# Between two transformer layers: batch 0's expert results are loaded first and added one by one, and TensorE projects batch 0 before it sums the other batches

## The chip, the cores and the metric

The kernel runs on one core of one Trainium2 chip, as a single program. The metric is the device time of that program in microseconds (us). Five engines run their own instruction streams in order and meet at semaphores: TensorE (PE in the profile, with its weight loads as PEld), VectorE (DVE), ScalarE (ACT), GpSimd (POOL) and SyncE (SP), which only issues DMAs here. ACT and POOL issue DMAs too; DMAs of one issuing engine go into one queue.

## The reference

Two layers over 4 batches of 512 tokens with 256 channels, all in float32. Each layer normalises the tokens and adds attention and a mixture of experts to them:

```
x = L0_attn_hidden_states                         # [4, 512, 256]
xn = _layernorm(x)
x = x + attn0(xn) + ffn0(xn)    # 16 experts, top 4 of a softmax, plus a shared expert
xn = _layernorm(x)
x = x + attn1(xn) + ffn1(xn)    # 32 query heads of 8 channels on 8 key groups; 7 experts, top 3, plus a shared one
```

In layer 1 the fused projection of `xn` gives 256 query, 64 key and 64 value columns; each of the 8 groups has one key head of 8 channels, which serves 4 query heads: scores over 512 keys, softmax, weighted values.

## The kernel before, in words

Tokens live in `x`, 16 tiles of 128 tokens by 256 channels, four tiles to a batch. Products of two float32 operands are made from a high part and a remainder (`_hi`, `_lo`) in three matmuls (`mm3`, L543 to L546). Layer 0 ends with the routed experts: POOL scatters their weighted results, one row for each token and choice, into the DRAM tensor `yk[0]`, four choices k = 0 to 3 of 2048 rows each. Then comes the stretch that the change is about. The order in every engine's stream is written out by hand; nothing is scheduled.

**Loads of the results.** For each batch b, SP issues choices 0 and 1 (`load_results`, L347 and L365 to L367) and ACT choices 2 and 3 (L1167 to L1170) into `yg[0][b]`: 16 DMAs of 512 KB, eight in each queue, batch 0 first. All four of a batch count on one semaphore, `m_yg[b]`.

**Adding them to the tokens.** `combine0(b, bank)` (L1524 to L1536) does it on DVE. Batch 0 takes four adds of 128 x 1024 elements, after all four loads have landed. For batches 1 to 3 DVE adds choice 0, TensorE adds up choices 1 to 3 with identity matmuls in two PSUM banks (`sum_results`, L912 to L919, 6 matmuls), and DVE adds the banks to the tokens (L1321). In TensorE's stream `sum_results(1)` stands ahead of the transposes of batch 0, `sum_results(2)` ahead of its two first projections and `sum_results(3)` behind them (L921 to L931).

**Normalising.** For each batch DVE takes moments (`moments`, L1283 to L1289), POOL a power (`root`, L437), DVE five small steps (L1296 to L1300), ACT writes four normalised tiles (`normalised`, L1007), TensorE transposes them (`tokens_t`, 8 transposes at L553, into the banks of `xt_bank`), ACT casts the high part (`high_parts`, L997) and DVE the remainder (`low_parts`, L1307).

**First projections and keys.** `project(2, 0)` gives batch 0's keys and values, `project(0, 0)` the queries of groups 0 to 3 (six matmuls each, L544 to L546). `compact` copies them out on ACT (L1186 to L1191) and DVE (L1673, L1676). SP then copies keys and queries inside SBUF into the form in which the scores want them: `stack_keys(u)` is four DMAs of 24 rows (L380) and `stack_queries(u)` one of 96 rows (L393), for each unit u, which is one key group of one batch.

**Units.** `stage(b, s)` is written once for each engine. Stage (0, 0) is the first unit of batch 0: 16 score matmuls (L815), each followed by a maximum on DVE (`reduce_max`, L1721) that frees its bank; a score waits for the maximum of the third score before it. Between these 16 steps stands what the dictionary `early` names for a step: in stage (0, 0) the transposes of batches 1 to 3, the last projection of batch 0 (`project(1, 0)`), `combine0`, `moments`, `root` and `low_parts` of batches 1 to 3. Behind the 16 steps follow the gate logits of all four batches (`logits`, six matmuls each, copied out by ACT and transposed in `logits_by_token`, L570); DVE takes them (`take_logits`, L1316), and then the second unit, stage (0, 1), begins with its first score. From there on units follow each other to the end of layer 1's attention, then its experts.

Of the kernel before, what the change touches and what calls it, by code (L numbers as in the profile page):

```python
# [41 lines left out]
def program(nc, x_in, aw0_in, aw1_in, ws0_in, moe0_in, moe1_in, pad_in, const_in, bias_in, out):  # L42
# [3 lines left out]
    with ctx:  # L46
# [179 lines left out]
        m_yg, m_fin = [sem(f"m_yg{b}") for b in range(B)], sem("m_fin")  # L226

# [17 lines left out]
        def batches(l, n):  # L245
            return n + l * B
# [76 lines left out]
        def _(sp):  # L323
# [23 lines left out]
            def load_results(l, b, k):  # L347
                r = k * T + b * S
                sp.dma_start(yg[l][b][:, k], yk[l][r:r + S, :].rearrange("(p t) h -> p t h", t=QT)).then_inc(m_yg[b], 16)
# [15 lines left out]
            for b in range(B):  # L365
                load_results(0, b, 0)
                load_results(0, b, 1)  # L367

            def stack_keys(u):
# [9 lines left out]
                for r in range(R):  # L379
# [45 lines left out]
        def _(pool):  # L425
# [61 lines left out]
            def add_results(b):  # L487

                pool.wait_ge(m_yg[b], 16 * (TOP0 + TOP1))
# [52 lines left out]
        def _(pe):  # L542
# [369 lines left out]
            def sum_results(b, bank):  # L912

                pe.wait_ge(m_yg[b], 16 * TOP0)
                for c in range(2):
                    for k in range(1, TOP0):
                        ins = nc.tensor.matmul(psum[:, bank + c, :], ident, yg[0][b][:, k, 2 * c:2 * c + 2, :],
                                               start=(k == 1), stop=(k == TOP0 - 1))
                ins.then_inc(m_ps, 1)  # L919

            sum_results(1, 4)  # L921
            tokens_t(1, 0)
            sum_results(2, 6)
# [4 lines left out]
            pe.wait_ge(s_ve, B + 2)  # L928
            sum_results(3, 4)
            pe.wait_ge(b_hi, 1)  # L930
            tokens_t(1, 1)  # L931
# [4 lines left out]
            def first_values():  # L936
# [3 lines left out]
            stage(0, 0, False, {1: lambda: pe.wait_ge(s_xl, 2 * B + 4), 3: last_projection, 7: lambda: tokens_t(1, 2),  # L940
                                11: lambda: tokens_t(1, 3), 12: first_values})
            pe.wait_ge(s_xl, 2 * B + 8)
            for b in range(B):
                logits(1, b, psum[:, 4 + b, :])
# [50 lines left out]
        def _(act):  # L995
# [171 lines left out]
            for b in range(B):  # L1167
# [53 lines left out]

            normalised(1, 0)
            high_parts(1, 0)
            normalised(1, 1)
# [664 lines left out]
```

## Time and profile before

| | us |
|---|---|
| runs shown | 1116.78, 1118.92, 1118.95 |
| median of the runs | 1118.92 |
| the profiled execution, its own time | 1118.09 |
| its span, first to last instruction | 1116.3 |
| from the first load of results to the first score of unit 0 | 384.57 to 423.01 |
| from that score to the first score of unit 1 | 423.01 to 457.74 |

All times of the trace are us from the start of the span. In a row of the timeline the first two numbers are start and duration, then engine, line of the kernel, operation, what it writes and reads, how many were merged, and in brackets how long the engine had been idle and what ended that. An engine that is idle costs nothing unless what it does next is waited for; so a stretch is read from its end backwards, always to what released it last.

### The profile page before, as it was taken

How to read it: one execution, taken by the hardware profiler on the slowest of the kernel's cores; microseconds unless marked ns; L12 is line 12 of the kernel's file. 1: busy time of each engine (PE TensorE's matmuls, PEld its weight loads, DVE VectorE, ACT ScalarE, POOL GpSimd, SP SyncE). 2: the span in 40 equal slices, each digit the busy share in tenths (PEclk: the TensorE clock that was granted, in tenths of full speed). 3: DMA queues.
4: the chain of work that ended last, by engine and by line, in shares of the span. 5: the costliest groups of instructions: out<-in, count | busy, mean ns of one | idle time of the engine just before them, and what ended most of it. 6: DMA issues, size and time to landing. Idle time of an engine off the chain costs nothing.

```text
span 1116.3 us, 17223 instructions
## 1 busy us (share of the span) xinstructions
PE 1004.6 (90%) x5701; PEld 735.6 (66%) x5701; DVE 762.9 (68%) x1575; ACT 591.3 (53%) x894; POOL 315.5 (28%) x330
## 2 busy tenths in 40 slices
PE   4999998789999575999999999999999987999996
PEld 3877876689999533555545555555555565888885
DVE  6577556566655257799898888888888756444438
ACT  6325553565555453466655665666566655444431
POOL 2004777256744400000000122222221000455432
PEclk9999998899999886999999999999999998999998
DMA  6863333655344352121111222222222124333244
GB/s 235 308 277 127 104 128 110 206 160 157 122 135 134 129 238 34 18 34 28 22 29 29 44 57 58 57 57 57 57 57 44 64 83 149 110 106 105 86 175 174
DMA packets 48962, 120.20 MB, mean 108 GB/s; under 512 B 7736, under 2 KB 24760, under 8 KB 48344
## 3 DMA queue, kind: packets, MB, share of 16 engines
q1 hardware_dynamic: 18960, 66.15, 20.3%
q0 software_dynamic: 11760, 32.24, 7.6%
q10 hardware_dynamic: 18160, 20.71, 6.5%
q8 instruction: 51, 0.84, 0.3%
q14 instruction: 31, 0.25, 0.1%
HBM read 72.17 MB, written 52.29 MB: 111 GB/s over the span
## 4 chain that ended last, share of the span: by engine, by line
PE 66%; DVE 14%; POOL 6%; ACT 5%; DMA 4%; issue 3%; SPq 0%; ACTq 0%; DVEq 0%; POOLq 0%
PE psum L815 11%; PE psum L837 10%; PE psum L824 8%; PE psum L630 5%; PE psum L631 4%; PE psum L632 4%; POOL xg L462 4%; DVE work_f L1721 4%; PE psum L544 3%; PE psum L545 3%; PE psum L546 3%; PE psum L616 2%; PE psum L641 2%; ACT work_f L1214 1%; DVE x L1321 1%
## 5 line engine op out<-in xcount | busy, mean ns | idle before, releaser
L1721 DVE TENSOR_REDUCE work_f<-psum 128x1 f32<-128x512 f32 x512 | 334.9, 685 | 51.1 <-PE psum L815 49.7
L1214 ACT ACTIVATE work_f<-psum 128x1024 f32<-128x1024 f32 x172 | 168.9, 1023 | 111.9 <-PE psum L824 110.3
L815 PE MATMUL psum<-work_r 128*128 128x512 f32 x512 | 205.3, 440 | 20.0 <-DVE work_f L1721 7.1
L469 POOL DMA_INDIRECT yk<-yb,dest x133 | 129.2, 971 | 238.7 <-ACT yb L1060 209.9
L815 PEld LDWEIGHTS psum<-work_r 128*128 128x128 f32 x512 | 94.2, 190 | 131.5 <-DVE work_f L1721 75.8
L824 PE MATMUL psum<-qm,work_r 128*128 128x512 f32 x512 | 161.8, 398 | 4.2 <-ACT work_f L1214 2.7
L462 POOL DMA_INDIRECT xg<-xn,slot x112 | 108.3, 967 | 180.5 <-PE psum L853 152.3
L824 PEld LDWEIGHTS psum<-qm,work_r 128*128 128x128 f32 x512 | 93.6, 188 | 31.8 <-ACT work_f L1214 10.9
L630 PE MATMUL psum<-wexp,xbh 128*128 x266 | 101.6, 382 | 9.3 <-issue 4.3
L1214 ACT ACTIVATE pt<-psum 128x1024 f32<-128x1024 f32 x84 | 82.8, 1023 | 50.2 <-PE psum L824 49.3
L631 PE MATMUL psum<-wexp,xbh 128*128 x266 | 95.7, 360 | 0.0
L632 PE MATMUL psum<-wexp,xbl 128*128 x266 | 95.2, 358 | 0.0
L837 PE MATMUL psum<-work_f 128*32 128x512 f32 x688 | 89.1, 602 | 0.6 <-ACT work_f L1214 0.6
L1044 ACT ACTIVATE sgb<-psum 128x352 f32<-128x352 f32 (+1 forms) x67 | 34.6, 517 | 97.5 <-PE psum L632 94.1
L1492 DVE TENSOR_TENSOR xbl<-psum,xbh 128x512 fp32r<-128x512 f32 x67 | 46.0, 686 | 57.5 <-ACT xbh L997 57.5
L1060 ACT ACTIVATE yb<-psum,share 128x256 f32<-128x256 f32 x133 | 55.9, 471 | 47.6 <-PE psum L659 23.8
L458 POOL TENSOR_TENSOR xn<-const 128x16 f32<-128x16 f32 x7 | 1.5, 218 | 260.2 <-PE psum L853 186.3
L1503 DVE TENSOR_TENSOR hb<-sgb,psum 128x352 f32<-128x352 f32 (+1 forms) x67 | 39.0, 582 | 51.9 <-ACT sgb L1044 51.9
L630 PEld LDWEIGHTS psum<-wexp,xbh 128*128 128x128 f32 x266 | 51.5, 194 | 15.6 <-issue 11.9
L632 PEld LDWEIGHTS psum<-wexp,xbl 128*128 128x128 f32 x266 | 51.6, 194 | 5.0
L631 PEld LDWEIGHTS psum<-wexp,xbh 128*128 128x128 f32 x266 | 51.6, 194 | 3.7
L616 PE MATMUL psum<-const,xb 128*128 128x128 f32 x266 | 41.3, 278 | 12.4 <-DVE xbl L1492 8.3
(218 smaller groups left out, 2035.3 us busy)
## 6 DMA issues: line engine op xcount, KB each, us to landing
xb<-xg ACTq DMA_DIRECT2D x62, 258.0 KB
xg<-in_pad SPq DMA_DIRECT2D x1, 10320.0 KB
yg<-yk SPq DMA_DIRECT2D x20, 512.0 KB, 9.3
stage<-in_moe SPq DMA_DIRECT2D x16, 608.0 KB, 5.2
xg<-in_pad SPq DMA_DIRECT2D x1, 7224.0 KB
work_r<-work_r SPq DMA_DIRECT2D x128, 48.0 KB
work_r<-work_r SPq DMA_DIRECT2D x32, 192.0 KB
stage<-in_moe SPq DMA_DIRECT2D x16, 384.0 KB, 3.8
```

What stands on the lines that cost most here:

```text
L462: nc.gpsimd.indirect_dma_start(xg[l], bass.IndirectOffsetOnAxis(ap=slot[l][:, at:at + 1], axis=0), xn[l][:, t, :], None).then_inc(m_scat, 16)
L469: nc.gpsimd.indirect_dma_start(yk[l], bass.IndirectOffsetOnAxis(ap=dest[:, j % 8, i:i + 1], axis=0), yb[l][:, j % 2, i, :], None).then_inc ...
L616: ins = nc.tensor.transpose(psum[:, 4, (i * KH + c) * P:(i * KH + c + 1) * P], xb[l][:, j % 2, i, c * P:(c + 1) * P], ident)
L630: nc.tensor.matmul(o, xbh[l][:, j % 2, i * KH + c, :], hi, start=c == 0, stop=False)
L631: nc.tensor.matmul(o, xbh[l][:, j % 2, i * KH + c, :], lo, start=False, stop=False)
L632: ins = nc.tensor.matmul(o, xbl[l][:, j % 2, i * KH + c, :], hi, start=False, stop=c == KH - 1)
L815: nc.tensor.matmul(next_bank(pe, ("scores", n), b_mx, n + 1), qs[g % 2][:, t * P:(t + 1) * P], km[g % 4][:, r, :], start=True, stop=True). ...
L824: ins = nc.tensor.matmul(psum[:, 3 + 2 * h + r % 2, :], km[g % 4][:, r, t * P:(t + 1) * P], qm[g % 2], start=True, stop=True)
L837: ins = nc.tensor.matmul(psum[32 * r:32 * r + 32, 7, :], va[:, t, g % NG * 32:g % NG * 32 + 32], pt[(n * QT + t) % 3][:, r, :], start=(t = ...
L1060: ins = nc.scalar.activation(yb[l][:, j % 2, i, :], psum[:, 6 + j % 2, i * H:(i + 1) * H], ACT.Identity, scale=share[:, j % 8, i:i + 1])
L1214: nc.scalar.activation(pt[((b * NG + g) * QT + t) % 3][:, 2 * h:2 * h + 2, :], psum[:, 3 + 2 * h:5 + 2 * h, :], ACT.Exp, scale=float(HD) * ...
L1721: v.reduce_max(mx[:, s % 2, i:i + 1], ring["scores", n], AX.X).then_inc(b_mx, 1)
```

## The change

SP and ACT issue the four loads of batch 0 with a semaphore for each choice (`m_y0[k]`). SP waits for choice 0 of them, and then issues all twelve loads of batches 1 to 3 itself. DVE adds batch 0's four in the order 0, 2, 1, 3, each when it has landed (`combine_first`). TensorE transposes and projects batch 0 first; then, for each of the other batches, it adds the tokens and all four choices in PSUM, in two halves of five identity matmuls (`sum_half`), and ACT copies the sum back over the tokens (`take_sum`), so DVE adds nothing for them. Batch 1's halves stand behind the projections, those of batches 2 and 3 between the scores of unit 0. Two of the four key copies of the first unit are issued by ACT. The logits move from behind unit 0 to its steps 13 and 15, except those of batch 3.

```diff
-            return ((0, 2), (3, 0), (6, 7), (4, 5))[b][k] if layer == 1 else 2 * b + k
+            return ((0, 2), (4, 5), (6, 7), (4, 5))[b][k] if layer == 1 else 2 * b + k
...
-            for b in range(B):
-                load_results(0, b, 0)
-                load_results(0, b, 1)
+            load_results(0, 0, 0)
+            load_results(0, 0, 1)
+            sp.wait_ge(m_y0[0], 16)
+            for b in range(1, B):
+                for k in range(TOP0):
+                    load_results(0, b, k)
...
-                for r in range(R):
+                for r in range(R if u else 2):
...
+            def sum_half(b, bank, c):
                 pe.wait_ge(m_yg[b], 16 * TOP0)
+                tokens = slice(b * QT + 2 * c, b * QT + 2 * c + 2)
+                nc.tensor.matmul(psum[:, bank + c, :], ident, x[:, tokens, :], start=True, stop=False)
+                for k in range(TOP0):
+                    ins = nc.tensor.matmul(psum[:, bank + c, :], ident, yg[0][b][:, k, 2 * c:2 * c + 2, :],
+                                           start=False, stop=(k == TOP0 - 1))
+                if c == 1:
+                    ins.then_inc(m_ps, 1)
...
+            def sum_last(c):
+                pe.wait_ge(s_xl, 2 * B + 4)
+                sum_half(3, 4, c)
...
-            stage(0, 0, False, {1: lambda: pe.wait_ge(s_xl, 2 * B + 4), 3: last_projection, 7: lambda: tokens_t(1, 2),
-                                11: lambda: tokens_t(1, 3), 12: first_values})
+            stage(0, 0, False, {0: lambda: sum_half(2, 6, 0), 1: lambda: sum_half(2, 6, 1), 2: lambda: tokens_t(1, 1),
+                                3: last_projection, 4: lambda: sum_last(0), 5: lambda: sum_last(1),
+                                7: lambda: tokens_t(1, 2), 10: lambda: tokens_t(1, 3),
+                                12: first_values, 13: first_logits, 15: third_logits})
...
-            for b in range(B):
-                for k in (2, 3):
-                    r = k * T + b * S
-                    act.dma_start(yg[0][b][:, k], yk[0][r:r + S, :].rearrange("(p t) h -> p t h", t=QT)).then_inc(m_yg[b], 16)
+            for k in (2, 3):
+                act.dma_start(yg[0][0][:, k], yk[0][k * T:k * T + S, :].rearrange("(p t) h -> p t h", t=QT)).then_inc(m_y0[k], 16)
...
+            def take_sum(b, bank):
+                act.wait_ge(m_ps, sums(0, b))
+                copy(x[:, b * QT:(b + 1) * QT, :].rearrange("p t h -> p (t h)"),
+                     psum[:, bank:bank + 2, :].rearrange("p c n -> p (c n)")).then_inc(s_cp, 1)
...
+            def combine_first():
+                dve.wait_ge(f_y, batches(0, B))
                 dve.wait_ge(s_xb, TT)
+                for k in (0, 2, 1, 3):
+                    dve.wait_ge(m_y0[k], 16)
                     noted()
+                    note(v.tensor_tensor(x[:, 0:QT, :], x[:, 0:QT, :], yg[0][0][:, k], ALU.add))
                 noted()
...
-            stage(0, 0, False, {1: lambda: low_parts(1, 1), 2: lambda: combine0(2, 6), 3: lambda: moments(1, 2),
-                                4: lambda: root(1, 2),
-                                6: lambda: combine0(3, 4), 7: lambda: moments(1, 3), 8: lambda: root(1, 3),
-                                9: lambda: compact(1, 0, psum[:, 3, :], 2), 10: lambda: low_parts(1, 2),
-                                13: lambda: low_parts(1, 3), 14: lambda: values_by_key(0, psum[:, 3, :])})
+            stage(0, 0, False, {0: lambda: summed_moments(1), 1: lambda: root(1, 1), 3: lambda: low_parts(1, 1),
+                                4: lambda: summed_moments(2), 5: lambda: root(1, 2),
+                                6: lambda: compact(1, 0, psum[:, 3, :], 2), 7: lambda: summed_moments(3),
+                                8: lambda: root(1, 3), 9: lambda: low_parts(1, 2),
+                                12: lambda: low_parts(1, 3), 14: lambda: values_by_key(0, psum[:, 3, :])})
```

TensorE's stream from the end of layer 0's experts to the first score, before (L917 is a sum of results, L553 a transpose of batch 0 or 1, L544 to L546 the projections, L815 a score):

```order
L917 MATMUL psum<-yg_1_129,const 128x512 [waits m_yg1,m_y]
L917 MATMUL psum<-yg_1_129,const 128x512 x5
L553 MATMUL psum<-const,xn_71 128x128 [waits s_xn]
L553 MATMUL psum<-const,xn_71 128x128 x7
L917 MATMUL psum<-yg_2_130,const 128x512 [waits m_yg2]
L917 MATMUL psum<-yg_2_130,const 128x512 x5
L544 MATMUL psum<-xt_hi_67,aw_73 128x512 [waits s_xl,s_split]
L545 MATMUL psum<-xt_lo_69,aw_73 128x512
...
L917 MATMUL psum<-yg_3_131,const 128x512 [waits m_yg3,s_ve]
L917 MATMUL psum<-yg_3_131,const 128x512 x5
L815 MATMUL psum<-work_r_146 128x512 [waits b_qd,b_kd]
```

The same place now (L558 transposes, L549 to L551 project, L921 and L923 are the sums, L820 a score):

```order
L558 MATMUL psum<-const,xn_71 128x128 [waits s_xb,s_xn,f_y,m_y]
L558 MATMUL psum<-const,xn_71 128x128 x7
L549 MATMUL psum<-xt_hi_67,aw_73 128x512 [waits s_xl,s_split]
L550 MATMUL psum<-xt_lo_69,aw_73 128x512
...
L921 MATMUL psum<-x,const 128x512 [waits m_yg1]
L923 MATMUL psum<-yg_1_129,const 128x512 x4
L820 MATMUL psum<-work_r_146 128x512 [waits b_qd,b_kd]
L921 MATMUL psum<-x,const 128x512 [waits m_yg2]
L923 MATMUL psum<-yg_2_130,const 128x512 x4
L820 MATMUL psum<-work_r_146 128x512
L558 MATMUL psum<-const,xn_71 128x128 [waits s_xn]
```

The sums moved from ahead of batch 0's transposes and projections to behind them, and batches 2 and 3 into unit 0. ACT's stream from the loads on, now (L1188 loads results, L1017 casts or copies, L1027 normalises, L1204 to L1209 copy projections out, L1252 copies keys):

```order
L1188 DMA yg_0_128<-yk 128x1024 [waits m_st1,m_st0,s_split]
L1207 ACTIVATE work_f_147<-psum,bias 128x512 [waits b_pj]
L1209 ACTIVATE work_r_146<-psum,bias 128x512 x2
L1204 ACTIVATE work_r_146<-psum,bias 128x512 [waits b_pj]
L1204 ACTIVATE work_r_146<-psum,bias 128x512
L1252 DMA work_r_146<-work_r_146 24x1x512 [waits b_km,b_lo]
L1252 DMA work_r_146<-work_r_146 24x1x512
L1017 COPY x<-psum 128x1024 [waits m_ps]
L1027 ACTIVATE xn_71<-x,rs 128x256 [waits s_nm]
L1027 ACTIVATE xn_71<-x,rs 128x256 x3
L1017 COPY x<-psum 128x1024 [waits m_ps]
```

Before, the four normalised tiles of batch 1 stood ahead of the first of these copies of projections (L1007 ahead of L1189); now they stand behind both, behind the two key copies and behind the first copy of a sum.

## Rows read from the trace of the kernel before

**Rows 1.** The page, part 2: busy tenths of TensorE, 40 slices of 27.9 us

```profile
PE   4999998789999575999999999999999987999996
```

**Rows 2.** Busy time by stretch: us, each engine's busy (instructions), granted TensorE clock, DMA share, GB/s

```profile
392.87:397.88 5.01, 0.00 (x0) 0.03 (x1) 4.90 (x4) 4.41 (x3) 0.00 (x0) 0.50 1.02 417
397.88:401.40 3.52, 3.52 (x4) 1.48 (x5) 2.23 (x11) 0.00 (x0) 1.04 (x1) 0.50 1.04 425
...
429.10:444.00 14.90, 6.59 (x18) 3.29 (x16) 13.29 (x40) 6.47 (x12) 2.01 (x2) 0.72 0.11 15
444.00:449.70 5.70, 5.65 (x20) 4.56 (x21) 5.35 (x10) 1.17 (x2) 0.00 (x0) 0.52 0.00 0
449.70:457.70 8.00, 6.99 (x38) 5.49 (x36) 1.42 (x5) 3.62 (x5) 0.00 (x0) 1.00 0.00 0
```

**Rows 3.** Timeline from the loads of results to the projections of batch 0

```profile
384.57 4.13 SPq L349 DMA_DIRECT2D yg<-yk  x8
...
392.87 5.00 DVE L1531 TENSOR_TENSOR x<-x,yg 128x1024 f32<-128x1024 f32 x4 [16.02 <-DMA yg<-yk]
...
397.88 7.26 PE L917 MATMUL psum<-yg,const 128*128 128x512 f32 x12 [20.02 <-DMA yg<-yk]
...
402.08 2.08 ACT L1007 ACTIVATE xn<-x,rs 128x256 f32<-128x256 f32 x4 [4.79 <-DVE rs L1300]
...
404.98 1.04 PE L553 MATMUL psum<-const,xn 128*128 128x128 f32 x8
...
406.44 1.29 DVE L1307 TENSOR_TENSOR xt_lo<-psum,xt_hi 128x512 fp32r<-128x512 f32 x2
...
410.61 0.80 PE L544 MATMUL psum<-xt_hi,aw 128*128 128x512 f32 x1
...
413.80 5.31 PE L917 MATMUL psum<-yg,const 128*128 128x512 f32 x12
```

**Rows 4.** SP's loads of results: issue to landing; then GB/s in the first 20 us (40 slices)

```profile
DMA to landing us min/median/max: 4.5/11.9/18.5
...
GB/s 0 0 0 66 246 303 377 410 426 426 385 377 426 401 409 413 413 409 503 399 466 433 389 357 412 430 418 412 350 41 0 0 0 0 0 0 0 0 0 0
```

**Rows 5.** Timeline from the first copies of projections to the first score

```profile
413.76 0.66 ACT L1189 ACTIVATE work_f<-psum,bias 128x512 f32<-128x512 f32 x1
...
415.61 0.69 DVE L1676 TENSOR_TENSOR work_r<-work_f,work_r 128x512 fp32r<-128x512 f32 x1 [3.87 <-ACT work_r L1191]
416.33 2.93 SPq L380 DMA_DIRECT2D work_r<-work_r  x4
...
419.35 0.64 SPq L393 DMA_DIRECT2D work_r<-work_r  x1
...
423.01 1.19 PE L815 MATMUL psum<-work_r 128*128 128x512 f32 x2 [3.03 <-DMA work_r<-work_r]
```

**Rows 6.** Timeline of unit 0 to the first score of unit 1

```profile
427.20 0.63 PE L545 MATMUL psum<-xt_lo,aw 128*128 128x512 f32 x1
...
427.63 0.63 PE L546 MATMUL psum<-xt_hi,aw 128*128 128x512 f32 x1
...
429.40 1.39 DVE L1283 BATCH_NORM_STATS2 st<-x 128x6 f32<-128x256 f32 x4
...
433.52 2.07 ACT L1007 ACTIVATE xn<-x,rs 128x256 f32<-128x256 f32 x4 [12.86 <-DVE rs L1300]
...
435.65 1.97 PE L553 MATMUL psum<-const,xn 128*128 128x128 f32 x8 [0.71 <-ACT xn L1007]
...
444.05 1.97 PE L553 MATMUL psum<-const,xn 128*128 128x128 f32 x8 [0.76 <-ACT xn L1007]
...
448.42 0.79 PE L544 MATMUL psum<-xt_hi,aw 128*128 128x512 f32 x1
...
457.74 0.97 PE L815 MATMUL psum<-work_r 128*128 128x512 f32 x3 [0.37 <-DVE lg L1316]
```

**Rows 7.** The page, part 5: ScalarE on 128 x 1024 elements out of PSUM

```profile
L1214 ACT ACTIVATE work_f<-psum 128x1024 f32<-128x1024 f32 x172 | 168.9, 1023 | 111.9 <-PE psum L824 110.3
```

More of the change, by code:

```diff
@@ L226, in program @@
         m_yg, m_fin = [sem(f"m_yg{b}") for b in range(B)], sem("m_fin")
+        m_y0, s_cp = [sem(f"m_y0_{k}") for k in range(TOP0)], sem("s_cp")
         def pairs(l, n):
@@ L348, in load_results @@
                 r = k * T + b * S
[L349 removed]
+                landed_on = m_y0[k] if l == 0 and b == 0 else m_yg[b]
+                sp.dma_start(yg[l][b][:, k], yk[l][r:r + S, :].rearrange("(p t) h -> p t h", t=QT)).then_inc(landed_on, 16)
             for e in range(9):
@@ L908, in sequence @@
                     stage(b, s, last)
-            def sum_results(b, bank):
+            def sum_half(b, bank, c):
                 pe.wait_ge(m_yg[b], 16 * TOP0)
[L915 to L921, printed above, removed]
+                tokens = slice(b * QT + 2 * c, b * QT + 2 * c + 2)
[5 more added lines that the diff above has]
+                    ins.then_inc(m_ps, 1)
+            pe.wait_ge(f_y, batches(0, B))
+            pe.wait_ge(s_xb, TT)
             tokens_t(1, 0)
-            sum_results(2, 6)
             pe.wait_ge(s_split, SPLIT_A1)
@@ L927, in _, with first_logits, third_logits @@
             project(0, 0, psum[:, 2, :])
[L928 to L931, printed above, removed]
+            sum_half(1, 4, 0)
+            sum_half(1, 4, 1)
+            def sum_last(c):
+                pe.wait_ge(s_xl, 2 * B + 4)
+                sum_half(3, 4, c)
+            def first_logits():
+                pe.wait_ge(s_xl, 2 * B + 6)
+                logits(1, 0, psum[:, 6, :])
+                logits(1, 1, psum[:, 7, :])
+            def third_logits():
+                pe.wait_ge(s_lt, B + 1)
+                logits(1, 2, psum[:, 6, :])
             def last_projection():
@@ L1233, in _ @@
             for b in range(B):
-                logits(1, b, psum[:, 4 + b, :])
+                logits(1, b, psum[:, 6 + b % 2, :])
             stage(0, 1, False)
@@ L1522, in routed, with summed_moments @@
                     weights(j)
-            def combine0(b, bank):
-                dve.wait_ge(f_y, batches(0, b + 1))
+            def combine_first():
+                dve.wait_ge(f_y, batches(0, B))
                 dve.wait_ge(s_xb, TT)
-                dve.wait_ge(m_yg[b], 16 * TOP0)
-                tiles = slice(b * QT, (b + 1) * QT)
-                for k in range(1 if b else TOP0):
+                for k in (0, 2, 1, 3):
+                    dve.wait_ge(m_y0[k], 16)
                     noted()
-                    note(v.tensor_tensor(x[:, tiles, :], x[:, tiles, :], yg[0][b][:, k], ALU.add))
-                if b:
-                    dve.wait_ge(m_ps, sums(0, b))
-                    noted()
-                    note(add_to_tokens(tiles, bank))
+                    note(v.tensor_tensor(x[:, 0:QT, :], x[:, 0:QT, :], yg[0][0][:, k], ALU.add))
                 noted()
+            def summed_moments(b):
+                dve.wait_ge(s_cp, b)
+                moments(1, b)
             def combine1(b):
@@ L1651, in _ @@
             dve.wait_ge(a_y, B + 1)
-            combine0(0, 0)
+            combine_first()
             moments(1, 0)
             root(1, 0)
-            combine0(1, 4)
             low_parts(1, 0)
-            moments(1, 1)
-            root(1, 1)
             def value_columns(c0, c1):
```

15 lines of the change are left out of this document (11 added, 4 removed).

## The prediction, made before the changed kernel ran

> **What bounds the kernel now.** I read the busy tenths first. TensorE is busy nearly everywhere; the dip to 5, 7 and 5 in slices 14 to 16 (363 to 446 us) is where the change is [rows 1]. Next I read the timeline of that dip, backwards from the first score of unit 1 at 457.74, which waits for DVE to take the gate logits [rows 6]. What feeds it is a chain through every engine. Results land, the last after 392.87; DVE adds batch 0 until 397.87; ACT normalises from 402.08; TensorE transposes at 404.98, and DVE's remainders end at 407.73. But the projections start only at 410.61, as twelve sums of batch 2 stand ahead of them [rows 3]. ACT copies the first one out only at 413.76, behind its normalising of batch 1; four key copies take SP from 416.33 on, the query copy goes out at 419.35, and the first score starts 3.66 later [rows 5]. Then unit 0 takes 34.7 us, with the last transposes at 444.05 and the logits from 448.42 on [rows 6]; DVE is busy 13.29 of 14.90 us there, TensorE 6.59 [rows 2]. So DVE and the chain of one batch after another bound that part, not TensorE.
>
> **Part 1: loads and adds.** Batch 0's transfers stand first in both queues already. SP's quickest result landed 4.5 us after its issue [rows 4]; three more of 0.524 MB at the 417 GB/s that flow there [rows 2] take 3.8, together 8.3, and the first add starts 392.87 - 384.57 = 8.3 after the first issue [rows 3]. So sending batch 0 out alone is worth nothing (bounds 0 and 1 us). What gains is that the adds no longer wait for all four. The add of choice 0 can start at about 389.4, and that of choice 2 follows. The first two end at 391.9. The last result lands at 392.87; when the third lands no row shows, and after it two adds of 1.25 remain. So the end is between 394.1 (one add left after 392.87) and 395.4 (two). I take 394.7, which is 3.2 earlier than 397.87.
>
> Batches 1 to 3 now come through SP's queue alone, issued from about 389.3, when SP's new wait for choice 0 ends; only these loads stand behind that wait. Twelve issues of 0.52 us [rows 3] take 6.2. SP's queue alone carried 380 to 430 GB/s in the kernel's first microseconds [rows 4], so 6.3 MB need 15 us: batch 1 is there by 398, batch 3 by 408, before anyone wants it.
>
> **Part 2: to the first projections.** From the last add to ACT's first normalised tile it takes 402.08 - 397.87 = 4.21, the four tiles 2.08 [rows 3]: 401.0. The transposes then start at once, where before they stood 0.8 behind the sums. But those sums had warmed TensorE. After its idle 20 us the granted clock was 0.50, the lower level of 1.2 GHz, and still so over the first four sums [rows 2]; now the transposes come first. At that level eight transposes take 1.97 [rows 6] and not 1.04 [rows 3]. Before, 2.75 passed from their start to the end of the remainders; I take 3.3. The projections start at 404.4, not at 410.61.
>
> Twelve projections cost (413.80 - 410.61) = 3.2 us at the full clock [rows 3], and 0.43 each, 5.2 in all, at half clock (427.20 to 427.63) [rows 6]. TensorE has hardly run until then, so I take half clock but for the last few: the first six end at 407.1, the second six at 409.3. At the full clock throughout, the first score would come 2 us sooner.
>
> The Trainium skill ("TensorE: Matmul & The Clock Gate", section "Part 1: The HAM clock gate") says that the array is throttled by default and that activity releases it. That speaks against putting the sums last, and by that rule, with which the row at 0.50 agrees, the slow prices above stand; without it the sum would come out about 2.5 us earlier.
>
> **Part 3: keys, queries, first score.** ACT no longer has batch 1's tiles ahead. From its start to DVE's compaction it is 415.61 - 413.76 = 1.85, then 0.69 [rows 5]: keys are ready at 409.7, not 416.3. SP issues two key copies (half of 2.93) until 411.2; the queries need ACT's copies of the second projection (1.25) and 0.75 on DVE: 411.4. The first score follows 3.66 after the query's issue [rows 5]: 415.1, which is 7.9 earlier than 423.01. ACT's own two issues (1.5 us, from 410.6) end at 412.1, before the sum that ACT waits for next.
>
> In TensorE's stream batch 1's ten sums stand ahead of that score: 0.44 each at full clock (5.31 for 12) [rows 3], 4.4, so 409.4 to 413.8. The wait for the queries hides them; at the 0.88 of the first four sums [rows 2] they would end at 418.2 and cost 3.1.
>
> **Part 4: unit 0.** DVE loses four passes of 1.25 over batches 2 and 3, and gains moments and root of batch 1, about 3 us. TensorE gains twenty sums (8.8 us) between scores. ACT gains three copies, 1.02 each by [rows 7], and batch 1's four tiles. DVE's moments now wait for ACT's copies, and behind them on DVE stand the maxima that free the scores' banks; so scores and sums of a later batch wait too. One batch hangs on the other: ACT's copy of the sum, then 433.52 - 429.40 = 4.12 from the moments to the first tile, 2.07 for the tiles, then transposes, casts, remainders [rows 6]. Batch 1: copy until 414.9, tiles 419.0 to 421.1; batch 2's sums end at about 420. Batch 2: ACT copies at 421.1 to 422.1, casts until 423.3, DVE's remainders until 424.6, then moments; tiles 428.7 to 430.8. Batch 3's ten sums wait for batch 1's remainders, 424.5 to 429 with their scores. ACT copies the last projection (1.25) and then this sum, until 433.1; moments from 433.6, tiles 437.7 to 439.8. So the last transposes start at 439.9, 4.2 before 444.05: of the 7.9 us, 3.7 go back.
>
> **Part 5: tail.** From the last transposes to unit 1 it was 13.7, of which 24 logit matmuls took 6.3 from 448.42 on [rows 6]. Now: transposes 1.97, three scores and the values 1.7, twelve logits 3.15, two scores 0.5, twelve logits 3.15, copy 0.7, then 2.34 as before: 453.3. With the first twelve at half clock, as the last transposes ran (clock 0.52) [rows 2], it is 455.3. I take 454.0 against 457.74: **3.7 us earlier**. Behind it nothing is changed, so the shift is carried to the end.
>
> The profiled execution took 1118.09, which gives 1114.4. The median of the runs is 0.83 higher, so I predict **1115.2**. With 0.7 either way in part 1, 2 us of clock in parts 2 and 3 and 2 in part 5, of which unit 0's chain hides some, its own range is 1113.0 to 1117.5.
>
> **Rivals.**
>
> *Slower: TensorE stays at 1.2 GHz.* Unit 0 has it idle for long (6.59 of 14.90 us busy, clock 0.72) [rows 2], and the change puts more matmuls on the chain. At half clock all through: batch 1's sums end at 418.2 and the first score stands there; batch 2's sums end near 428, its copy and batch 1's transposes behind them, batch 3's sums near 440.5, last transposes near 449.9, and the tail takes some 19 with 10.4 for the logits: 469, or 12 us slower, 1131. It decides from about 4 us of such losses on: batch 3's sums at half clock (4.4) alone eat the gain, 1119.9. Against it: the sums themselves keep TensorE busy, and before the change the transposes behind twelve of them already ran at the fast price (1.04) [rows 3]. Chance 0.09.
>
> *No change: given back in unit 0.* If unit 0 hangs wholly on ACT and DVE, the earlier first score is worth less than I think. ACT has batch 1's and 2's tiles, two copies and the last projection in one line; one more wait of a tile set (2.07) behind a copy or a maximum leaves 1.6 us: 1117.3. For it: DVE's 13.29 of 14.90. Chance 0.20.
>
> *The loads come late.* With SP's queue at half the rate, 6.3 MB would last until 420, and the keys and queries of unit 0 stand behind them in that queue: first score at 423 as before, and the unit 3.7 longer: 1122.6. Rows 4 speak against it. Chance 0.03. The Trainium skill ("DMA: Bandwidth & Descriptors", section "Queues, rings and completion order") says that every DMA engine takes turns between the queues that have work. Batch 1's loads, issued while choices 1 and 3 still flow, would then take turns with ACT's choice 3; no row here shows a queue that joins late, and the cost would fall inside the 1 us in which I let the third and fourth land.
>
> *More: the clock comes up early and stays.* The 2 us of part 2, 0.7 of part 1 and the fast tail add up to a first score of unit 1 at 451 or before: 1112 or less. Chance 0.07.
>
> **How the numbers follow.** The forecast has 0.61, the rivals 0.09, 0.20, 0.03 and 0.07. About 0.2%, 2.2 us, is what a measurement of this kernel can tell from none. Faster: nine tenths of the forecast (0.55), all of the large gain (0.07) and a third of the second rival (0.07): 0.69. Slower: 0.03, three quarters of the first rival (0.07) and a little of the second (0.01): 0.11. The rest, 0.20, is the same. From 1112.3 to 1119.0 leaves out the late loads, most of the half clock and the largest gains, not quite 2 in 10.
>
> **What would show it.** In the profile of the changed kernel, in each case against the times above: the last add of batch 0 near 394.7; the projections near 404.4 and at 0.43 apart at first; the first score near 415, released by a DMA inside SBUF; last transposes near 440, that is 25 us after the first score and not 21; unit 1 near 454; and everything behind it shifted by as much. I am wrong on the mechanism if the first score waits for sums or for loads, and on the size if the last transposes come 21 us or 29 us after it.

## The result: slower by 0.4%, and the profile after

The changed kernel takes **1122.65 us** (median of 19 runs, 1118.14 to 1128.49), the kernel before 1118.30 in the same comparison (19 runs). The ratio is 1.0039 with an interval of 1.0027 to 1.0052. Forecast were 1115.2 us and 3.7 us of gain; measured are 4.4 us of loss.

The profiled execution of the changed kernel, 1128.49 us, is the longest of its 19, so its stretches are read one by one and not its total. Counted from the first load of layer 0's results, which shuts out what layer 0 does before it, the profiles of before and after say (us):

| | before | forecast | after |
|---|---|---|---|
| last add of batch 0 | 13.3 | 10.1 | 10.2 |
| transposes of batch 0 start | 20.4 | 16.4 | 16.6 |
| projections start | 26.0 | 19.8 | 20.1 |
| first key copy issued | 31.8 | 25.1 | 25.6 |
| first score of unit 0 | 38.4 | 30.5 | 33.4 |
| last transposes (batch 3) | 59.5 | 55.3 | 62.3 |
| first score of unit 1 | 73.2 | 69.4 | 75.3 |
| from there to layer 1's first load of results | 620.5 | 620.5 | 620.3 |
| from that load to the end | 38.0 | 38.0 | 43.4 |

The span is 10.3 us longer: 3.0 ahead of the first load, where nothing is changed, 2.15 up to unit 1, -0.2 in the long middle, and 5.4 at the end. The 2.15 and the 5.4 have each a cause of their own. That is more than the 4.4 us of the medians, so the terms are those of one execution.

The rows that answer to [rows 3] and [rows 5] show the first half of the table. The timeline of VectorE and of TensorE after the change, with start, duration, engine, line, operation, tiles, count, and the idle time ahead with its releaser:

```profile
392.35 2.55 DVE L1560 TENSOR_TENSOR x<-x,yg 128x1024 f32<-128x1024 f32 x2 [13.38 <-DMA yg<-yk]
395.22 2.56 DVE L1560 TENSOR_TENSOR x<-x,yg 128x1024 f32<-128x1024 f32 x2 [0.31 <-DMA yg<-yk]
```

```profile
404.20 1.94 PE L558 MATMUL psum<-const,xn 128*128 128x128 f32 x8 [24.11 <-ACT xn L1027]
407.63 0.77 PE L549 MATMUL psum<-xt_hi,aw 128*128 128x512 f32 x1 [1.49 <-DVE xt_lo L1337]
408.20 0.63 PE L550 MATMUL psum<-xt_lo,aw 128*128 128x512 f32 x1
408.63 0.63 PE L551 MATMUL psum<-xt_hi,aw 128*128 128x512 f32 x1
```

The adds start 4.8 after the first load and wait only 0.31 between; the transposes take 1.94 and the projections start 0.43 apart, which is the half clock that was forecast. The next rows, TensorE's timeline of the sums of batches 1 and 2, show what was not:

```profile
412.75 1.02 PE L921 MATMUL psum<-x,const 128*128 128x512 f32 x2
...
413.61 3.60 PE L923 MATMUL psum<-yg,const 128*128 128x512 f32 x8
...
417.04 1.02 PE L921 MATMUL psum<-x,const 128*128 128x512 f32 x2
...
417.90 3.60 PE L923 MATMUL psum<-yg,const 128*128 128x512 f32 x8
...
420.94 0.79 PE L820 MATMUL psum<-work_r 128*128 128x512 f32 x1
...
421.57 1.02 PE L921 MATMUL psum<-x,const 128*128 128x512 f32 x2
422.42 3.60 PE L923 MATMUL psum<-yg,const 128*128 128x512 f32 x8
425.46 0.80 PE L820 MATMUL psum<-work_r 128*128 128x512 f32 x1
426.09 1.02 PE L921 MATMUL psum<-x,const 128*128 128x512 f32 x2
426.95 3.60 PE L923 MATMUL psum<-yg,const 128*128 128x512 f32 x8
429.98 0.79 PE L820 MATMUL psum<-work_r 128*128 128x512 f32 x1
430.61 1.04 PE L558 MATMUL psum<-const,xn 128*128 128x128 f32 x8
```

Batch 1's two halves have 5 matmuls each in the code (the tokens and four results) and 2 + 8 instructions each in the trace: a plain float32 matmul is **two** instructions, each 0.43 long at full clock. Ten sums are 20 instructions and 8.65 us, not 4.4. The first score stands behind them without an idle time of its own, each of the next two scores waits for a half of batch 2, and batch 1's transposes wait for all of it, until 430.61. The table of stretches (length, busy time and count of PE, PEld, DVE, ACT and POOL, clock, DMA share, GB/s) says the same against [rows 2]:

```profile
412.75:421.40 8.65, 8.65 (x22) 3.86 (x21) 2.71 (x6) 1.27 (x2) 0.00 (x0) 1.00 0.34 51
...
429.10:444.00 14.90, 14.90 (x54) 8.39 (x52) 8.36 (x24) 6.64 (x12) 1.01 (x1) 1.00 0.04 6
```

From 429.1 to 444.0 the kernel before had TensorE busy for 6.59 of 14.90 us and VectorE for 13.29 [rows 2]. Now TensorE is busy for all of it, at full clock, and VectorE for 8.36. TensorE has become the bound of this part of unit 0. The page's tenths [rows 1], slices of 28.2 us now, have slices 14 to 16 at 4, 5, 8 instead of 5, 7, 5: the two in which the first results land and are added (366 to 422 us) are emptier than before, that of unit 0 (422 to 451) is fuller. The last slice is at 5 instead of 6:

```profile
PE   4999998689999458999999999999999978999995
```

The second loss is at the end. These are stretches of 6 us in layer 1, 12 to 18 and 18 to 24 us behind its first load of results; first the kernel before, then the changed one:

```profile
1090.25:1096.25 6.00, 5.94 (x32) 4.93 (x31) 5.85 (x6) 1.12 (x2) 4.27 (x2) 1.00 1.00 406
1096.25:1102.25 6.00, 6.00 (x39) 5.34 (x38) 5.96 (x6) 1.12 (x2) 2.67 (x1) 1.00 0.03 12
```

```profile
1095.19:1101.19 6.00, 4.44 (x24) 3.35 (x23) 6.00 (x2) 0.00 (x0) 4.62 (x2) 1.00 0.83 340
1101.19:1107.19 6.00, 5.09 (x18) 4.22 (x19) 5.96 (x9) 2.21 (x4) 2.37 (x1) 0.72 0.22 89
```

VectorE is busy for the same 6 us, but in the first of the two stretches with two instructions instead of six; TensorE waits, then runs at a granted clock of 0.72. None of this code is changed, but for the counts of semaphores. What is changed is its neighbour: the trace's DMA records hold 16 KB fetches of instructions on queue 8, 51 before and 52 now. One falls 8.7 us behind layer 1's first load of results before, and 2.9 us behind it now. The second and third result then land at 5.45 and 7.21 us instead of 4.74 and 6.00, and GpSimd's first add starts at 7.3 instead of 6.07.

### The profile page after: what moved, and what is told of

It reads as the page before. It is cut to its first block, busy times and chain, and to the rows that moved or that the text cites. A ratio compares the mean times of both kernels' runs of the same rounds, so it can differ in the third digit from the quotient of the medians.

```text
span 1126.6 us, 17262 instructions
## 1 busy us (share of the span) xinstructions
PE 1012.8 (90%) x5725; PEld 739.7 (66%) x5725; DVE 757.9 (67%) x1569; ACT 594.8 (53%) x897; POOL 316.4 (28%) x330
## 4 chain that ended last, share of the span: by engine, by line
PE 67%; DVE 13%; POOL 7%; ACT 5%; DMA 4%; issue 4%; SPq 0%; ACTq 0%; DVEq 0%; POOLq 0%
PE psum L820 10%; PE psum L842 10%; PE psum L829 8%; PE psum L635 5%; PE psum L636 4%; PE psum L637 4%; POOL xg L467 4%; DVE work_f L1747 4%; PE psum L549 3%; PE psum L550 3%; PE psum L551 3%; PE psum L646 2%; PE psum L621 2%; PE psum L923 2%; DMA yg<-yk 1%
## 5 line engine op out<-in xcount | busy, mean ns | idle before, releaser
L820 PE MATMUL psum<-work_r 128*128 128x512 f32 x512 | 204.4, 437 | 10.4 <-DVE on L1718 4.9
L820 PEld LDWEIGHTS psum<-work_r 128*128 128x128 f32 x512 | 93.4, 188 | 120.6 <-DVE work_f L1747 69.0
L1232 ACT ACTIVATE pt<-psum 128x1024 f32<-128x1024 f32 x84 | 82.9, 1024 | 50.2 <-PE psum L829 49.3
```

The source lines that it names most:

```text
L820: nc.tensor.matmul(next_bank(pe, ("scores", n), b_mx, n + 1), qs[g % 2][:, t * P:(t + 1) * P], km[g % 4][:, r, :], start=True, stop=True). ...
L1232: nc.scalar.activation(pt[((b * NG + g) * QT + t) % 3][:, 2 * h:2 * h + 2, :], psum[:, 3 + 2 * h:5 + 2 * h, :], ACT.Exp, scale=float(HD) * ...
```

## The experiments

Two theories for the first loss: TensorE's row is too long (a sum costs twice what was counted), or the first unit hangs on VectorE and ScalarE. Two for the second: the place of the instruction fetch, or what the change computes. Each ratio is to the kernel before on the same chip; the differences of stretches are to the first profiles of the two kernels. Sums in the reduced type were not measured, so the price of a sum is tested by its place and by fewer sums alone.

**The changed kernel again, unaltered.**

> The changed kernel itself, to see what of its profile comes back. Theory A (a sum on TensorE costs 0.88 us and not the 0.44 that the prediction took, because a float32 matmul is two instructions): the first score again waits for batch 1's sums, about 30.3 us from the first score's wait-free time on, and from the first load of results to unit 1 about 75 us; the rest of the kernel as before the change. Then the time is 1119 to 1122. Rival B (something in the last 45 us, behind layer 1's experts, has become 5 us slower for good): the last stretch is 5 us longer in this profile too.

Measured: 1124.67 us, ratio 1.0049 (1.0032 to 1.0066). Unit 1 at 74.4 us behind the first load, the end stretch 43.4 again. Both losses repeat, the first one smaller: the first score comes at 32.7 and not 33.4, unit 1 1.2 us behind the kernel before and not 2.15 (the third profile, further down, has 32.8 and 74.4). The 3.0 us ahead of the first load do not repeat (1.1 here).

**The loads alone**: the kernel before with batch 0's loads sent out by themselves. The edit in short:

```
+ m_y0 = [sem(f"m_y0_{k}") for k in range(TOP0)]     # batch 0: one semaphore per choice
+ load_results(0, 0, 0); load_results(0, 0, 1); sp.wait_ge(m_y0[0], 16)
+ for b in range(1, B): all four choices by SP       # ACT loads only choices 2, 3 of batch 0
+ DVE adds batch 0 in the order 0, 2, 1, 3, each after its own semaphore
```

> The kernel before with the first part of the change alone: four semaphores for batch 0, its adds in the order 0, 2, 1, 3, and batches 1 to 3 loaded by SP. The step of the prediction on loads and adds: the last add of batch 0 ends 10.2 us after the first load instead of 13.3. Theory A says nothing more comes of it, because TensorE's sums of batch 1 stand ahead of batch 0's transposes and cannot start before batch 1 has landed: transposes within 0.5 us of before, time 1117.5 to 1119. Rival D (the earlier adds alone carry the gain): 3 us sooner at every later step, time 1115 to 1116.

Measured: 1119.82 us, ratio 1.0008 (0.9997 to 1.0020). The adds end at 10.2 us as in the changed kernel, yet the transposes start at 21.95 us instead of 20.4, later than even theory A allowed. TensorE's timeline of this kernel shows why:

```profile
399.03 7.78 PE L922 MATMUL psum<-yg,const 128*128 128x512 f32 x12 [21.06 <-DMA yg<-yk]
406.65 1.04 PE L558 MATMUL psum<-const,xn 128*128 128x128 f32 x8
407.52 5.32 PE L922 MATMUL psum<-yg,const 128*128 128x512 f32 x12
```

Batch 1's sums stand ahead of the transposes, and batch 1 lands 1.0 later behind the first load than before (the sums then take 7.78 instead of 7.26), so what the adds gain is lost again. Loads and order belong together.

**Batch 1 added by VectorE**: the changed kernel, with batch 1's four results added by VectorE while it waits for keys, and one half of batch 2's sum ahead of the first score.

```
- sum_half(1, 4, 0); sum_half(1, 4, 1)               # TensorE, ahead of the first score
+ sum_half(2, 6, 0)
- stage(0, 0, False, {0: sum_half(2, 6, 0), 1: sum_half(2, 6, 1), 2: tokens_t(1, 1), ...
+ stage(0, 0, False, {0: sum_half(2, 6, 1), 2: tokens_t(1, 1), ...
+ combine_second()                                   # DVE: four adds, after low_parts(1, 0)
```

> As the changed kernel, but batch 1's four results are added by DVE, 5 us in the time in which it otherwise waits for the copies of the first projection, and batch 1's moments follow those copies; TensorE does batch 2's first half where batch 1's sums stood. Theory A: 8.8 us of sums less on TensorE before the first score, one copy less on ACT; first score about 28 us after the first load, batch 1's tiles 8 us earlier, unit 1 at 67 to 70 us after the first load, time 1113 to 1116. Rival C: no gain over the changed kernel beyond 1 us, as DVE bounds unit 0.

Measured: 1118.30 us, ratio 0.9994 (0.9982 to 1.0005); unit 1 at 72.3 us, the end stretch 38.2, the fetch at 7.0 us. Ten matmuls fewer take unit 1 from 75.3 (74.4 in the other two profiles) to 72.3. That is short of theory A's 67 to 70, and so is the time; and of the gain over the changed kernel the end stretch has the larger part (5.2 us in the profiles). The first score was to come at 28 and came at 32.4, only 1.0 earlier, though TensorE stood idle ahead of it:

```profile
411.45 3.60 PE L923 MATMUL psum<-yg,const 128*128 128x512 f32 x8
418.67 0.47 PE L820 MATMUL psum<-work_r 128*128 128x512 f32 x1 [3.62 <-DMA work_r<-work_r]
418.98 1.18 PE L921 MATMUL psum<-x,const 128*128 128x512 f32 x2
419.96 5.17 PE L923 MATMUL psum<-yg,const 128*128 128x512 f32 x8
```

So the score waits for the query copy, and the second half of the sum stands behind the score when it could lie in that 3.62.

**Both halves ahead of the first score**: the kernel just told of, with the half moved into the gap.

```
  sum_half(2, 6, 0)
+ sum_half(2, 6, 1)
- stage(0, 0, False, {0: sum_half(2, 6, 1), 2: tokens_t(1, 1), ...
+ stage(0, 0, False, {1: tokens_t(1, 1), ...         # DVE's steps 3, 4, 5 one earlier
```

> Batch 1's results are added by VectorE, as in the run before it, and both halves of batch 2's sum now stand ahead of the first score, batch 1's transposes after the first score instead of the second. Theory (a sum costs TensorE 0.88 us, so a batch's ten sums 8.8 us, and whatever stands behind them in TensorE's row is late by what sticks out of the wait for the query): the 4.3 us of the second half fit into the 3.6 us in which TensorE waits for the query, so the first score is at most 0.7 us later, batch 1's transposes start 4 to 5 us earlier (about 34.5 us after the first load of results instead of 39.2), unit 1 at 68 to 70 us after that load instead of 72.3, and the kernel takes 1113.5 to 1116 us. Rival (the first unit is bound by VectorE's and ScalarE's work and not by TensorE's row): unit 1 stays at 72 us and the time at 1118 us.

Measured: **1111.61 us**, ratio 0.9952 (0.9935 to 0.9970), the fastest version. It beats the kernel before by 0.5% and the changed one by 0.9%, the latter in part by the end stretch (37.4 us). The first score is no later (32.4 us), unit 1 comes at 66.2, earlier than the theory's 68 to 70, and the time is below its range too:

```profile
413.05 1.02 PE L921 MATMUL psum<-x,const 128*128 128x512 f32 x2
413.91 3.60 PE L923 MATMUL psum<-yg,const 128*128 128x512 f32 x8
416.95 1.02 PE L820 MATMUL psum<-work_r 128*128 128x512 f32 x2
418.19 1.09 PE L558 MATMUL psum<-const,xn 128*128 128x128 f32 x8 [0.22 <-ACT xn L1027]
```

Batch 1's transposes start 33.7 us behind the first load; in the changed kernel it was 43.1. The 10 matmuls taken off TensorE and the place of five are worth 9.1 us at unit 1 (8.2 against the other two profiles): the theory of TensorE's row holds, the rival (72 us) falls.

**Two results fewer in each sum.**

```
-                for k in range(TOP0):
+                for k in range(2):
```

> The changed kernel with choices 2 and 3 left out of TensorE's sums of batches 1 to 3, so that three matmuls make a half instead of five (the results of these two choices are missing from those batches' tokens). Theory (0.88 us for a sum at full clock): batch 1's sums take 5.3 us instead of 8.8, the first score comes 3 to 3.5 us earlier (about 30 us after the first load instead of 33.4), batch 1's transposes 5 to 7 us earlier, unit 1 at 69 to 71.5 us instead of 75.3. Rival (0.44 us for a sum, as the prediction had it, and something else that holds up the first score): the first score less than 1.8 us earlier. TensorE's row is as long as the kernel's before to a few instructions, so by theory A of the fetch the stretch behind layer 1's first load of results is back at 38 us, by rival B it stays at 43; the whole 1112 to 1116 us, or 1118 to 1121.

Measured: 1114.40 us, ratio 0.9971 (0.9960 to 0.9982). Unit 1 at 70.7 and the end stretch 37.5, as the theory had them. The first score missed its figure: 1.1 us earlier, not 3 to 3.5, as the rival had it (under 1.8); and batch 1's transposes came 3.2 earlier, not 5 to 7. The rival's price of a sum does not hold all the same: the sums did take 3.3 us less (5.3 against 8.65). But the score then waited for the query copy:

```profile
416.22 0.47 PE L820 MATMUL psum<-work_r 128*128 128x512 f32 x1 [2.60 <-DMA work_r<-work_r]
```

From the issue of the first key copy to the first score it is 6.7 us before, 6.8 here and 6.8 with batch 1 added by VectorE, no matter that the key copies now go out by two queues at once; DMA moved 84 GB/s in this wait both before and here. In the changed kernel it is 7.8, and 7.2 to 7.3 in its other two profiles, so the sums hold up the first score by 0.4 to 1.0.

**The kernel before, with 50 idle instructions.** The cleanest test of the second loss, as nothing of the change is in it.

```
+            for _ in range(100):
+                pe.wait_ge(s_split, 1)     # long met; the profile counts 50 instructions more
             sum_results(1, 4)
```

> The kernel before with 100 waits for a semaphore that is long met (50 instructions, as many as the change adds) in TensorE's row ahead of the sums of batch 1, where TensorE waits for the loads; nothing else is changed. Theory A (position of the 16 KB fetch of instructions beside layer 1's first loads of results): the fetch falls 2.5 to 4 us after the first of these loads instead of 8.7, the first add of GpSimd starts at about 7.3 us instead of 6.05, the stretch from the first load to the end takes about 43.4 us instead of 38.0, and the kernel takes 1122.5 to 1125 us. Rival B (the loss belongs to what the change computes): 38 us and 1118 to 1119 us.

Measured: 1122.25 us, ratio 1.0031 (1.0018 to 1.0045), the fetch at 2.9 us, GpSimd's first add at 7.3, the end stretch 42.2 instead of 38.0: theory A, with 1.2 us less than its 43.4 and a median just under its range. The same 12 to 24 us of that stretch:

```profile
1088.26:1094.26 6.00, 4.45 (x24) 3.35 (x23) 6.00 (x2) 0.00 (x0) 4.59 (x2) 1.00 0.81 332
1094.26:1100.26 6.00, 5.11 (x18) 4.24 (x19) 5.96 (x9) 2.34 (x4) 2.38 (x1) 0.72 0.22 87
```

They are the changed kernel's rows almost to the digit: fifty instructions that do nothing make the second loss, but for 1.2 us of it: 30 to 37 us behind the load TensorE's granted clock is 0.68 in the changed kernel and 1.00 here. How a 1.2 us delay grows to 4 shows in VectorE's and GpSimd's timelines, first of the kernel before, then of this one (two fences each):

```profile
1086.85 0.69 DVE L1475 TENSOR_TENSOR hs_lo<-hhs,hs_hi 128x512 fp32r<-128x512 f32 x1
...
1088.05 1.22 DVE L1543 TENSOR_TENSOR x<-x,yg 128x1024 f32<-128x1024 f32 x1
1089.18 0.69 DVE L1475 TENSOR_TENSOR hs_lo<-hhs,hs_hi 128x512 fp32r<-128x512 f32 x1
1089.79 3.42 DVE L1543 TENSOR_TENSOR x<-x,yg 128x1024 f32<-128x1024 f32 x1
```

```profile
1084.32 2.39 POOL L490 TENSOR_TENSOR yg<-yg 128x1024 f32<-128x1024 f32 x1 [7.50 <-DMA yg<-yk]
1089.60 2.52 POOL L490 TENSOR_TENSOR yg<-yg 128x1024 f32<-128x1024 f32 x1 [2.88 <-DMA yg<-yk]
```

```profile
1084.84 1.65 DVE L1477 TENSOR_TENSOR hs_lo<-hhs,hs_hi 128x512 fp32r<-128x512 f32 x1
...
1088.15 2.88 DVE L1477 TENSOR_TENSOR hs_lo<-hhs,hs_hi 128x512 fp32r<-128x512 f32 x1
1090.96 3.41 DVE L1545 TENSOR_TENSOR x<-x,yg 128x1024 f32<-128x1024 f32 x1
```

```profile
1083.55 2.39 POOL L490 TENSOR_TENSOR yg<-yg 128x1024 f32<-128x1024 f32 x1 [8.72 <-DMA yg<-yk]
1087.23 3.25 POOL L490 TENSOR_TENSOR yg<-yg 128x1024 f32<-128x1024 f32 x1 [1.28 <-DMA yg<-yk]
1090.92 2.37 POOL L490 TENSOR_TENSOR yg<-yg 128x1024 f32<-128x1024 f32 x1 [0.44 <-DMA yg<-yk]
```

Before, the small subtraction `hs_lo` runs twice in 0.69: at 1086.85, when GpSimd's first add is over, and at 1089.18, ahead of the add of 1089.60. With the fetch moved the first add, 1.2 later, lies beside the first `hs_lo` (1.65), and the second starts 0.9 into the next add, which runs until 1090.48, and takes 2.88. The next pass over `x` meets an add in both kernels (3.42 before, 3.41 now, against 1.22 without one), so it adds nothing to the loss. The two subtractions, 0.96 and 2.19 longer, make the 3.15 us by which VectorE is late behind that pass. TensorE then waits 2.39, where before it had no such wait, and comes back to a falling clock. Its timeline in this kernel:

```profile
1095.15 0.50 PE L544 MATMUL psum<-xt_hi,wsh 128*128 128x512 f32 x1 [2.39 <-DVE hhs L1472]
...
1095.73 0.39 PE L546 MATMUL psum<-xt_hi,wsh 128*128 128x512 f32 x1
1095.96 0.40 PE L544 MATMUL psum<-xt_hi,wsh 128*128 128x512 f32 x1
...
1097.62 0.63 PE L546 MATMUL psum<-xt_hi,wsh 128*128 128x512 f32 x1
```

The Trainium skill ("SBUF — State Buffer", section "Who interferes with whom") says that a VectorE instruction with two inputs in SBUF and a GpSimd instruction that reads SBUF share a port, and that the later one is blocked until the first is done. These rows agree: 2.88 and 3.41 beside an add, 0.69 and 1.22 without.

**The changed kernel with its fetch moved back**, by 412 such waits (206 instructions), run twice, the second time beside the unaltered changed kernel on the same chip.

```
+            for _ in range(412):
+                pe.wait_ge(s_split, 1)
             pe.wait_ge(f_y, batches(0, B))
```

> The changed kernel with 412 waits for a semaphore that is long met (two to an instruction, so 206 instructions) in TensorE's row before batch 0's transposes, where TensorE waits for VectorE; nothing is computed otherwise. Together with the 48 instructions and one or two waits by which the changed kernel's row is longer, this is 256 instructions or 16 KB, one fetch of instructions. Theory A (the 5.4 us lost behind layer 1's first load of results come from a 16 KB fetch of instructions that falls beside the first loads, 2.9 us after the first of them): the fetch falls at 8 to 9 us after that load as in the kernel before, the stretch from there to the end takes 38 us instead of 43.4, and the kernel takes 1118 to 1120.5 us. Rival B (the loss comes from what the change computes or where, not from the fetch): the stretch stays at 43 us and the time at 1122 to 1125 us, or 2 us more for the added waits.

> The changed kernel with 412 waits (206 instructions), once more, for a second profile: the first one showed the stretch of 37.4 us that theory A asked for, and a median of 1122.2 us that it did not. Theory A: 37.4 to 38 us behind layer 1's first load, and a median below that of the unaltered changed kernel on this chip by 2 to 5 us. Rival C: as above. Whatever else is late shows between the stretches: first load of layer 0's results, unit 1, first load of layer 1's results.

> The changed kernel unaltered, beside the same kernel with its fetch moved, on the same chip. Theory A: its stretch behind layer 1's first load of results is 43 us again and its time 2 to 5 us above that of the one with the fetch moved. Rival C (the long stretch belongs to some executions only, and the two kernels differ by no more than their spread): the two medians within 1.5 us, and a stretch of 38 us in one of the changed kernel's profiles or of 43 us in one with the fetch moved.

Measured: both profiles of the moved kernel have the fetch at 8.5 to 8.7 us and an end stretch of 37.4; the changed kernel's third profile has 3.0 and 43.4 again. In the moved one, the stretches 12 to 24 us behind the load are those of the kernel before:

```profile
1090.80:1096.80 6.00, 5.94 (x32) 4.94 (x31) 5.86 (x6) 1.12 (x2) 4.30 (x2) 1.00 1.01 414
1096.80:1102.80 6.00, 6.00 (x39) 5.35 (x38) 5.96 (x6) 1.12 (x2) 2.87 (x1) 1.00 0.03 12
```

The medians follow only in part. On one chip, 1120.04 (ratio 1.0020, 1.0009 to 1.0031) against 1122.66 unaltered (1.0037, 1.0023 to 1.0052): 2.6 us back, with intervals that overlap. In the first run, on another chip, 1122.17 (1.0035, 1.0023 to 1.0046), well above what theory A asked for, although its one profile has the short stretch; unit 1 came at 76.0 us in it, at 74.1 in the second. The profiled executions of the changed kernel (1128.49, 1125.34, 1125.51) all lie above their medians, those of the moved one (1120.81, 1118.00) below. So rival C, that only some executions have the long stretch, is not ruled out for the executions that were not profiled. The mechanism is shown in every profile; its share in the medians, 0.5 us (1122.17 against 1122.65), 2.6, or 3.5 by the fifty idle instructions, is not settled.

**The fetch elsewhere**: the fastest version with 92 waits, and the changed kernel with 180, at the same place.

> The version with both halves of batch 2's sum ahead of the first score, with 92 waits for a semaphore long met (46 instructions) added to TensorE's row before batch 0's transposes. Theory A (position of the 16 KB fetch of instructions): the fetch moves from 7.2 us behind layer 1's first load of results to about 3 us, the stretch from that load to the end grows from 37.4 to 42 or 43 us, and the time from 1111.6 us to 1114.5 to 1117 us; unit 1 stays at 66 to 67 us after the first load of layer 0. Rival B (the stretch is long for another reason): 37.4 us and 1111 to 1112.5 us.

> The changed kernel with 180 such waits (90 instructions) in TensorE's row before batch 0's transposes. Theory A: the 16 KB fetch falls 2 to 5 us ahead of layer 1's first load of results, where it meets no load of results; GpSimd's first add starts at 6.05 us again and the stretch to the end takes 38 us, unless the next fetch, then 22 to 28 us behind that load, does harm of its own; 1118 to 1121 us. Rival B: 43 us, 1122 to 1125 us.

Measured: the first 1114.42 us (0.9968, 0.9953 to 0.9982), 2.8 us above the version without the waits, with intervals that overlap; but the fetch came at 0.6 us and not at 3, and the end stretch is 38.8, not 42. GpSimd's first add is late there too (7.7), yet the chain of collisions ends sooner. VectorE's pass over `x`, and GpSimd's add beside it:

```profile
1088.49 1.21 DVE L1580 TENSOR_TENSOR x<-x,yg 128x1024 f32<-128x1024 f32 x1
...
1088.62 3.34 POOL L495 TENSOR_TENSOR yg<-yg 128x1024 f32<-128x1024 f32 x1 [0.61 <-DMA yg<-yk]
```

Here the pass starts 0.13 ahead of the add and takes 1.21; with the 50 idle instructions it starts 0.04 behind it (1090.96 against 1090.92) and takes 3.41. Being late alone does not decide; by these rows, which of a pair starts first does.

The second 1123.78 us (1.0053, 1.0040 to 1.0067): the fetch is 8.6 us ahead of the load, not 2 to 5, and the end stretch 37.2 as theory A asked, but the 149.3 us from layer 1's first expert to that load have become 152.2; the time is a miss. The fetch meets no load there, but it meets the scatters of the last expert's results. One of them takes 4.3 us from issue to landing instead of 2.4, ScalarE's next copy for a scatter starts 0.07 behind that landing, as in the other traces, and the last scatters, which the load waits for, land 2.9 us late. So the stretch behind the load is short because the load is late: from the first expert to the end it is 189.4 us, against 192.7 in the changed kernel's third profile and 186.5 in the second one with the fetch moved back.

## Why the prediction was wrong

**Right**: part 1 (last add 10.2 against 10.1), part 2 (transposes and projections within 0.3, at half clock), the loads of batches 1 to 3 in time (batch 1 had landed 14.5 us behind the first load, its sums began at 25.2), the middle unchanged.

**The step that failed** is the price of a sum in parts 3 and 4: "batch 1's ten sums stand ahead of that score: 0.44 each at full clock (5.31 for 12) [rows 3], 4.4". The row is right and its count was misread: the 12 instructions are the six matmuls that one batch needed before, so 5.31 is the price of six, 0.88 each, and ten cost 8.65. In part 4, "TensorE gains twenty sums (8.8 us) between scores" should read 17.3, in a unit that took 34.7. By that, "DVE and the chain of one batch after another bound that part, not TensorE" ceased to hold. The prediction named its own signs of this: last transposes 29 us after the first score and not 25 (28.95 in all three profiles of the changed kernel), and, for a wrong mechanism, a first score that waits for sums, which it does for 0.4 to 1.0 us. It even had the right price in hand, as that of half clock: with 0.88 for a sum its batch 1 ended at 418.2, 33.6 us behind the first load, and the first score came at 33.4.

The Trainium skill ("FP8 and Floating Point Precision", section "TensorE Precision Notes") says that true float32 takes four passes through the array. The trace agrees in the price: 0.86 for 512 columns, where matmuls of split operands, in the reduced type, run 0.23 apart at full clock (1095.73 and 1095.96 above).

The 5.9 us between forecast and unit 1 in the first profile (5.0 in the other two), term by term: keys issued 0.5 later; key and query copies 1.4 longer, because "half of 2.93" was saved on the issue and not in the time from the first issue to the score (6.7 before, 6.8 now); 1.0 of sums that the wait for the query did not cover; 4.15 in unit 0; less 1.1, by which the part from the last transposes to unit 1 was shorter than forecast. Together 5.95.

**"Behind it nothing is changed, so the shift is carried to the end"** is the second failure. The middle did carry it. The end did not: 24 matmul instructions more, with as many weight loads and two waits, moved a fetch of instructions from 8.7 to 2.9 us behind a load of results, worth up to 5.4 us in a profile.

**The rivals.** The loads were not late. Unit 0 did give back more than was gained, but not on VectorE or ScalarE. The nearest was the first, by its place: TensorE becomes the bound of unit 0, with last transposes about 10 us later than forecast (7.0 measured). Its cause was wrong: the clock was 1.00 there, and it was the number of instructions that doubled. Two sums of this rival are off without weight: 469 is 11.3 us past 457.74, which gives 1130.2, and 4.4 on 1115.2 is 1119.6.

## What to carry to other kernels

Count instructions of a row against matmuls in the code before a duration is multiplied: plain float32 here has two to a matmul. When work moves onto an engine, add up that engine's busy time in the stretch after the move; where it fills the stretch, the engine is the bound, whatever bounded it before, and the place of each piece (in a wait or behind it) decides. And a change that lengthens an engine's instruction stream can move a loss into code that it does not touch: compare the end stretches, and pad the old kernel to test it.

## What was not expected of the hardware

Fifty idle instructions slowed the kernel before by 0.31%, through one 16 KB fetch beside loads of results (queue 8, 0.94 us in the records). Adding 256 instructions (206 idle ones, 48 of the change and two waits) brought the fetch back to 8.5 to 8.7 us. Where two instructions of VectorE and GpSimd met, VectorE's took 1.21 us where it started 0.13 ahead and 3.41 where it started 0.04 behind. And sending copies of the same size out by two queues did not bring the last one in sooner: 6.7 to 6.8 us from the first issue to the score, by one queue or two.
